# Attention weights turned on VectorE in squares of 32 and exchanged through DRAM, in place of TensorE transposes

## The chip, the cores and the metric

The kernel runs on one core of one Trainium2 chip, as one program. The metric is the device time of one execution in microseconds (us); the median of three executions is given.

## What is computed

The reference has two layers over a tensor x of 8 x 256 x 256 (batch, sequence, width). Layer 0 is a mixture of experts inside another one (two expert networks, A and B). Layer 1 is attention followed by a third expert network (D). The change lies in the attention alone:

```python
xn = layernorm(x, g_in)
q = (xn @ Wq).reshape(b, n, H, DH).transpose(0, 2, 1, 3) * scale      # 16 heads of 64
kv = xn @ Wkv                                                        # one key and value head for all
k = concatenate([nk, k], axis=1); v = concatenate([nv, v], axis=1)   # one null key in front
sim = einsum('bhid,bjd->bhij', q, k) + bias                          # bias: one 256 x 256 table per head
sim = where(causal_mask, neg, sim); sim = where(mask_p, sim, neg)
attn = softmax(sim, axis=-1)
out = einsum('bhij,bjd->bhid', attn, v)
return layernorm(out.reshape(b, n, INNER) @ Wo, g_out)
```

## The kernel before

Every instruction of every engine is written out by hand; engines meet through semaphores. The attention runs over 8 batches (b) and, in each, over 8 pairs of heads (j); p = 8b + j counts the 64 pairs. One pass of the inner loop is called a slot here: each engine has a fixed program for slot p, in `pe_batch`, `act_batch`, `dve_batch` and `pool_batch` (TensorE, ScalarE, VectorE, GpSimd).

A pair has two heads (o = 0, 1) and two blocks of 128 queries (i). Because of the causal mask the first block needs 129 keys (the null key and 128) and the second 257; a score row of both has 386 columns. The steps of a pair are these:

- `pe_queries` makes the queries of the pair (2 matmuls of 256 columns into psY), `act_queries` copies them to `c_qr`.
- `pe_scores` makes the scores (4 matmuls into psH), `dve_scores` adds the bias and mask tile `c_bm` (made by GpSimd in `pool_bm`) and takes the minimum of each row, for one head at a time (two custom instructions and two reads of the accumulator). The same kind of pass is done for the other head.
- `act_exp` makes the exponentials `c_p` and their sums. `dve_sums` takes reciprocals of the 4 sums per partition.
- The weighted sum over keys needs the weights with keys on partitions. `pe_turn` transposes three 128 x 128 pieces for each head on TensorE (psHT), `act_pT` and `dve_pT` copy them out, one head each, to `c_pT`.
- `dve_over` spreads the reciprocals over 64 columns for each head (`c_over`), and two more transposes in `pe_queries` turn them. They ride in the upper half of psY and of `c_qr`.
- `pe_sum` multiplies the values `c_v` with `c_pT` (4 matmuls into psL), `dve_o` multiplies by the turned reciprocals, and `pe_out` multiplies with `Wo` into psM (2 matmuls that add up over the pairs of a batch).

In slot p TensorE does sum(p-1), scores(p+1), turn(p), queries(p+2) with the turned reciprocals of p, out(p-1). Besides these, each slot of a batch has work of its own: row statistics and normalization of the next batch (slots 2 and 3), its keys and values (slots 5, 6), the output rows of the batch before, and the routing of network D (from batch 2 on). SP (SyncE) issues the loads; at the start of the attention it queues all weights of D and the zeroing of D's rows in DRAM.

## Time and profile before

| | us |
|---|---|
| median of 3 executions | 797.87 |
| lowest, highest | 794.5, 798.69 |
| span of the profiled execution, first to last instruction | 793.7 |
| attention, first slot to the last weighted sum (344.51 to 655.21) | 310.7 |

The time of the profiled execution itself is not listed apart from the three; its span lies 0.8 us under the fastest of them and 4.2 us under the median. In the rows below, "busy" is the time in which an engine had an instruction in its pipeline. Instructions of one engine overlap a little, so what one costs is read from the start of one to the start of the next.

### The profile page before, as it was taken

To read this page: it belongs to the slowest core of one execution; us is meant where nothing else is said; L and a number is where in the kernel's file an instruction comes from. 1 tells how busy PE (TensorE), PEld (TensorE's weight loads), DVE (VectorE), ACT (ScalarE), POOL (GpSimd) and SP (SyncE) were. 2 spreads that over 40 slices of the span, in tenths; PEclk is the share of its full clock that TensorE was granted. 3 is DMA by queue.
4 is the path that set the end of the run, shared out by engine and by line. 5 is a ranking of instruction groups with operands and counts; after the bars stand their busy time and mean duration, and the time that the engine had idled before them with its cause. 6 is when DMAs were issued, how large, how long until landed. Compare 5 with 4: busy or idle time off the path is not lost. (4 is left out here: it accounts for less than half of the span.)

```text
span 793.7 us, 16690 instructions
## 1 busy us (share of the span) xinstructions
PE 748.7 (94%) x4993; PEld 595.9 (75%) x4994; DVE 453.7 (57%) x1647; ACT 381.9 (48%) x1094; POOL 422.4 (53%) x506
## 2 busy tenths in 40 slices
PE   8889999769999999989999999999999988899998
PEld 4479966549999999867777777777777754699965
DVE  0824475672232323356666787778878787256557
ACT  3556612242222222166666565656666651777611
POOL 1077327525554852274656668686868356056640
PEclk9999999759999999999999999999999999999999
DMA  9636635429897773395000000000000001356547
GB/s 323 279 108 191 137 118 160 126 81 342 309 329 273 223 231 121 107 401 174 28 1 28 2 28 29 28 29 28 29 1 29 1 29 63 102 160 177 153 149 236
DMA packets 57022, 106.36 MB, mean 134 GB/s; under 512 B 8816, under 2 KB 42864, under 8 KB 55792
## 3 DMA queue, kind: packets, MB, share of 16 engines
q1 hardware_dynamic: 40368, 55.96, 20.9%
q0 software_dynamic: 10944, 30.03, 12.5%
q10 hardware_dynamic: 5632, 19.41, 7.2%
q8 instruction: 39, 0.64, 0.3%
q14 instruction: 39, 0.32, 0.1%
HBM read 78.31 MB, written 27.07 MB: 133 GB/s over the span
## 5 line engine op out<-in xcount | busy, mean ns | idle before, releaser
L2135 POOL TENSOR_TENSOR work<-work,region_ac 128x386 f32<-128x386 f32 x128 | 120.3, 945 | 67.2 <-DVE work L1797 32.7
L1683 ACT ACTIVATE work<-work 128x129 f32<-128x129 f32 (+1 forms) x256 | 114.0, 449 | 5.8 <-DVE work L1797 5.8
L1797 DVE CUSTOM_DVE_ANT_0 work<-psH,work 128x129 f32<-128x129 f32 (+1 forms) x256 | 78.8, 345 | 2.6 <-PE psH L1482 2.6
L1690 ACT COPY work<-psHT 128x384 f32<-128x384 f32 x64 | 30.6, 479 | 86.4 <-PE psHT L1492 86.4
L1355 POOL DMA_INDIRECT d_pairs<-work,home x47 | 46.1, 981 | 42.8 <-DVE home_f L1107 27.4
L1463 PE MATMUL psY<-work,region_ac 128*128 128x256 f32 x256 | 66.9, 384 | 0.5 <-ACT work L1677 0.5
L1516 PE MATMUL psM<-region_ac,work 128*128 128x256 f32 x256 | 66.0, 380 | 0.0
L1025 ACT ACTIVATE work<-work 128x512 f32<-128x512 f32 x39 | 24.6, 630 | 86.0 <-DVE work L1044 86.0
L1344 POOL DMA_INDIRECT b_pairs<-work,home x39 | 38.0, 975 | 49.8 <-DVE work L1051 46.8
L1336 POOL DMA_INDIRECT work<-in_x,inv x39 | 37.0, 949 | 47.0 <-DVE inv L1264 35.5
L848 PE MATMUL psH<-work,region_bd 128*128 128x128 f32 x472 | 59.2, 280 | 2.0 <-ACT region_bd L747 1.1
L1482 PE MATMUL psH<-region_bd,work 64*128 64x129 f32 (+1 forms) x512 | 59.4, 350 | 1.4 <-DVE work L1797 1.4
L848 PEld LDWEIGHTS psH<-work,region_bd 128*128 128x128 f32 x472 | 56.5, 196 | 2.8 <-ACT work L956 1.4
L1492 PEld LDWEIGHTS psHT<-ident,work 128*128 128x128 f32 x384 | 40.8, 141 | 21.2 <-issue 20.3
L1492 PE MATMUL psHT<-ident,work 128*128 128x128 f32 x384 | 56.1, 282 | 0.0
L1505 PE MATMUL psL<-work 128*64 128x256 f32 (+1 forms) x512 | 55.7, 339 | 0.1
L1336 POOL DMA_INDIRECT work<-y_scratch,inv x39 | 37.6, 965 | 32.2 <-DVE inv L1264 20.7
L1505 PEld LDWEIGHTS psL<-work 128*64 128x64 f32 x512 | 31.2, 136 | 30.3 <-issue 21.1
L1677 ACT ACTIVATE work<-psY 128x512 f32<-128x512 f32 (+1 forms) x66 | 38.5, 583 | 29.9 <-PE psY L1468 24.4
L1823 DVE TENSOR_TENSOR work<-psL,work 128x256 f32<-128x256 f32 x64 | 26.9, 421 | 44.6 <-PE psL L1505 44.3
L1417 POOL DMA_INDIRECT work<-a_slots,slot_u x32 | 31.1, 973 | 33.4 <-DMA a_slots<-work 23.9
L1683 ACT ACTIVATION_READ_ACCUMULATOR work<-work 128x1 f32 x256 | 48.7, 190 | 0.0
(368 smaller groups left out, 1694.6 us busy)
## 6 DMA issues: line engine op xcount, KB each, us to landing
region_bd<-in_b_w ACTq DMA_DIRECT2D x37, 512.0 KB, 5.4
work<-d_rows SPq DMA_DIRECT2D x47, 132.0 KB, 2.2
a_slots<-work SPq DMA_DIRECT2D x19, 256.0 KB, 2.9
region_bd<-in_b_w SPq DMA_DIRECT2D x1, 4096.0 KB, 15.3
work<-b_pairs SPq DMA_DIRECT2D x16, 256.0 KB, 3.1
region_bd<-in_d_w SPq DMA_DIRECT2D x1, 4096.0 KB, 13.2
work<-d_pairs SPq DMA_DIRECT2D x16, 256.0 KB, 4.3
d_rows<-region_bd SPq DMA_DIRECT2D x1, 2112.0 KB, 28.5
```

What stands on the lines that cost most here:

```text
L848: last = pe.matmul(pair_h[p % DEEP][:, t % PAIR, j, :], f.w_in(j, k, t), xT[:, p % DEEP, t % PAIR, k, :], start=(k == 0), stop=(k == KD - 1))
L1336: pool.indirect_dma_start(out=slot_rows(f, t), out_offset=None, in_=st.src, in_offset=bass.IndirectOffsetOnAxis(ap=inv[:, t:t + 1], axis=0 ...
L1355: pool.indirect_dma_start(out=st.pair_dram, out_offset=bass.IndirectOffsetOnAxis(ap=home[:, t:t + 1], axis=0), in_=d_ys[:, t % ROWS, :], i ...
L1463: last = pe.matmul(psY[:, 0:SEQ], c_wq[:, c, j * P:(j + 1) * P], c_xnT[:, odd, c, :], start=(c == 0), stop=(c == KD - 1))
L1482: last = pe.matmul(psH[:, o, a:z], c_qr[half, j % 2, i * P:(i + 1) * P], c_kT[half, 0:z - a], start=True, stop=True)
L1492: last = pe.transpose(psHT[:, o, n * P:(n + 1) * P], c_p[:, o, at:at + P], ident[:, :])
L1505: last = pe.matmul(psL[DH * o:DH * o + DH, queries], c_v[:, keys, :], c_pT[:, o, at], start=(n == 0), stop=(n == 1))
L1516: last = pe.matmul(psM[:, i * DIM:(i + 1) * DIM], c_oT[:, j % 2, i * P:(i + 1) * P], c_wo[:, j, :], start=(j == 0 and i == 0), stop=(j == ...
L1677: nc.scalar.mul(c_qr[:, j % 2, a:z], psY[:, a:z], -(float(DH) ** -0.5)).then_inc(C.qr_ready, 1)
L1683: nc.scalar.activation(c_p[:, o, a:z], c_sc[:, o, a:z], ACT.Exp, scale=-1.0, bias=c_min[:, o, i:i + 1], accum_out=c_sum[:, j % 2, o, i:i + ...
L1797: last = nc.vector.tensor_tensor_reduce(c_sc[:, o, a:z], psH[:, o, a:z], c_bm[:, 2 * (j % 2) + o, a:z], 1.0, -LOWEST, ALU.add, ALU.min, c_ ...
L2135: pool.tensor_tensor(c_bm[:, 2 * (j % 2) + o, :], c_mp, c_bias[:, 2 * j + o, :], ALU.subtract).then_inc(C.bm_ready, 1)
```

## The change

The six transposes of the weights, the two of the reciprocals, their PSUM banks and the copies out of PSUM go away. VectorE now turns squares of 32 x 32 within each group of 32 partitions (`dve_blocks`, one instruction of 384 columns for each head; `dve_recs`, 256 columns of reciprocals). This gives turned squares that still lie in the wrong group of partitions. One DMA writes the whole pair (4 KB per partition, 512 KB) to DRAM, and another reads it back so that the squares land in the right group (`sp_store_blocks`, `sp_load_blocks`). The keys are held in another order for this (every fourth key together), so bias and mask arrive permuted. The weighted sum comes three slots later (LAG = 3), scores have two banks instead of one (psH and psHT in turn), the heads are taken in the order 1, 0, and D's weights are loaded differently: `d_w13` by SP, the others by ScalarE's queue in the first twelve slots, `d_b2` after the attention, since its room holds the buffers `c_x1` and `c_x2`. Rows of pairs (`c_gat`) are now loaded by ScalarE's queue too.

```diff
@@ pe_queries
-            if live(k, -2, 1 << 30):
-                wait(pe, C.rec_ready, k - 1)
-                for i in range(QT):
-                    last = pe.transpose(psY[:, SEQ + i * P:SEQ + (i + 1) * P], c_over[:, i, :, :].rearrange("p o n -> p (o n)"),
-                                        ident[:, :])
@@ pe_turn
-        def pe_turn(pe, p):
-
-            for o in range(2):
-                pe.wait_ge(C.p_ready, 4 * p + 2 * o + 2)
-                wait(pe, C.pT_ready[o], p)
-                for n, at in enumerate((1, KEYS0 + 1, KEYS0 + 1 + P)):
-                    last = pe.transpose(psHT[:, o, n * P:(n + 1) * P], c_p[:, o, at:at + P], ident[:, :])
-                last.then_inc(C.p_turned, 1)
@@ pe_sum
-            for s in C.pT_ready:
-                pe.wait_ge(s, p + 1)
+            wait_dma(pe, C.blocks_loaded, 0, p)
@@ pe_batch
-                before = not (first and j == 0)
-                if before:
-                    pe_sum(pe, p - 1, (j - 1) % NPAIR, b - (j == 0))
+                s = p - LAG
                 if not (last and j == NPAIR - 1):
                     pe_scores(pe, p + 1, (j + 1) % NPAIR, b + (j + 1) // NPAIR)
-                pe_turn(pe, p)
+                if s >= 0:
+                    pe_sum(pe, s, s % NPAIR, s // NPAIR)
...
-                if before:
-                    pe_out(pe, p - 1, (j - 1) % NPAIR, b - (j == 0))
+                if s >= 0:
+                    pe_out(pe, s, s % NPAIR, s // NPAIR)
@@ act
-        def act_pT(act, p):
-            act.wait_ge(C.p_turned, 2 * p + 1)
-            wait(act, C.pv_mm, p)
-            nc.scalar.copy(c_pT[:, 0, :], psHT[:, 0, 0:3 * P]).then_inc(C.pT_ready[0], 1)
@@ dve
         def dve_sums(dve, p, j):
             dve.wait_ge(C.p_ready, 4 * p + 4)
-            nc.vector.reciprocal(c_rec, c_sum[:, j % 2, :, :]).then_inc(C.rec_done, 1)
-
-        def dve_over(dve, p):
+            wait(dve, C.blocks_turned, 3 * p)
+            nc.vector.reciprocal(c_rec, c_sum[:, j % 2, :, :].rearrange("p o i -> p i o").unsqueeze(3).to_broadcast([P, QT, 2, 16])
+                                 ).then_inc(C.rec_done, 1)
+
+        def dve_recs(dve, p):
+
 
             dve.wait_ge(C.rec_done, p + 1)
...
+            nc.vector.transpose(out=c_x1[:, p % 2, :, 2 * (QT + 1):, :].rearrange("p b i q -> p i b q"),
+                                in_=c_rec.rearrange("p i o n -> p i (o n)").unsqueeze(2).to_broadcast([P, QT, 4, 32])
+                                ).then_inc(C.blocks_turned, 1)
+
+        def dve_blocks(dve, p, j, o):
+
+
+            n = ORDER.index(o)
+            dve.wait_ge(C.p_ready, 4 * p + 2 * n + 2)
+            if p >= 2 and n == 0:
+                wait_dma(dve, C.blocks_stored, 0, p - 2)
+            nc.vector.transpose(out=c_x1[:, p % 2, :, (QT + 1) * o:(QT + 1) * (o + 1), :].rearrange("p b i q -> p i b q"),
+                                in_=c_p[:, j % 2, o, 1:1 + BLOCK].rearrange("p (i b q) -> p i b q", b=4, q=32)).then_inc(C.blocks_turned, 1)
@@ sp
+        def sp_store_blocks(sp, p):
+
+
+            r = p % 4
+            sp.wait_ge(C.blocks_turned, 3 * p + 3)
+            if p >= 4:
+                wait_dma(sp, C.blocks_loaded, 0, p - 4)
+            sp.dma_start(blocks_dram[r].rearrange("a (k b) m -> (a k) (b m)", b=4), c_x1[:, p % 2, :, :, :].rearrange("p b n q -> p (b n q)")
+                         ).then_inc(C.blocks_stored.sems[p % 2], 16)
+
+        def sp_load_blocks(sp, p):
+
+
+            r = p % 4
+            wait_dma(sp, C.blocks_stored, 0, p)
+            wait(sp, C.o_ready, p - 1)
+            sp.dma_start(c_x2[:, p % 2, :, :, :].rearrange("p a n q -> p a (n q)"), blocks_dram[r].rearrange("a s m -> s a m")
+                         ).then_inc(C.blocks_loaded.sems[p % 2], 16)
...
+            sp_clear_rows(sp)
+            sp.dma_start(d_w13, io["d_w13"]).then_inc(D.weights_loaded, 16)
+            pairs = NPAIR * BATCH
+            for p in range(pairs):
+                sp_store_blocks(sp, p)
+                if p >= 1:
+                    sp_load_blocks(sp, p - 1)
+            sp_load_blocks(sp, pairs - 1)
```

How the instructions stand on VectorE in a slot of the middle (slot 2 of a batch), before. "ISA" is the score pass of `dve_scores` and its accumulator reads; the names in brackets are the semaphores waited for.

```order
L1823 TENSOR_TENSOR work<-psL,work 128x256 [waits c_wo_mm,c_qr_ready,c_pv_mm]
L1803 RECIPROCAL work<-work 128x4 [waits c_p_ready,c_bm_ready,c_s_mm]
L1797 ISA work<-psH,work 128x129
L1797 ISA work 128x1
L1797 ISA work<-psH,work 128x257
L1797 ISA work 128x1
L1809 COPY region_bd<-work 128x256 [waits c_qr_mm,c_rec_done]
L1815 COPY work<-psHT 128x384 [waits c_p_turned,c_pv_mm,b_combined,c_out_step]
L1797 ISA work<-psH,work 128x129
L1797 ISA work 128x1
L1797 ISA work<-psH,work 128x257
L1797 ISA work 128x1
```

And the same place of the changed kernel, from the start of the slot to its second score pass.

```order
L1835 STREAM_TRANSPOSE region_bd<-work 128x3x4x32 [waits tokens_stored0,c_p_ready]
L1810 ISA work<-psHT,work 128x129 [waits c_p_ready,c_bm_ready,c_s_mm]
L1810 ISA work 128x1
L1810 ISA work<-psHT,work 128x257
L1810 ISA work 128x1
L1835 STREAM_TRANSPOSE region_bd<-work 128x3x4x32 [waits c_p_ready]
L1817 RECIPROCAL work<-work 128x64 [waits c_blocks_turned,c_p_ready]
L1824 STREAM_TRANSPOSE region_bd<-work 128x2x4x32 [waits c_rec_done]
L1844 TENSOR_TENSOR work<-psL,region_bd 128x256 [waits c_wo_mm,tokens_stored3,c_pv_mm]
```

The multiplication by the reciprocals (L1823, now L1844) moved from the start of the slot to behind the turning; the reciprocal has 64 columns instead of 4.

TensorE in one slot before, from the weighted sum to the output.

```order
L1505 MATMUL psL<-work 64x256 [waits c_o_ready,c_pT_odd,c_pT_even]
L1505 MATMUL psL<-work 64x256
L1505 MATMUL psL<-work 64x128 x2
L1482 MATMUL psH<-region_bd,work 128x129 [waits c_score_ready,c_kT_ready,c_qr_ready]
L1482 MATMUL psH<-region_bd,work 128x129
L1482 MATMUL psH<-region_bd,work 128x257 x2
L1492 MATMUL psHT<-ident,work 128x128 [waits c_pT_even,c_p_ready]
L1492 MATMUL psHT<-ident,work 128x128 x2
L1492 MATMUL psHT<-ident,work 128x128 [waits c_pT_odd,c_p_ready]
L1492 MATMUL psHT<-ident,work 128x128 x2
```

TensorE in one slot of the changed kernel, from the scores to the output, which is the last thing of the slot.

```order
L1487 MATMUL psHT<-region_bd,work 128x129 [waits c_score_ready,c_qr_ready]
L1487 MATMUL psHT<-region_bd,work 128x129
L1487 MATMUL psHT<-region_bd,work 128x257 x2
L1500 MATMUL psL<-region_bd,work 64x256 [waits c_o_ready,tokens_stored3]
L1500 MATMUL psL<-region_bd,work 64x256
L1500 MATMUL psL<-region_bd,work 64x128 x2
L1473 MATMUL psY<-work,region_ac 128x256 [waits c_qr_ready]
L1473 MATMUL psY<-work,region_ac 128x256
L1511 MATMUL psM<-region_ac,work 128x256 [waits c_o_ready]
L1511 MATMUL psM<-region_ac,work 128x256
```

The scores now stand ahead of the weighted sum, and right behind the output of the slot before, which waits for VectorE's `dve_o` (c_o_ready).

## Rows read from the trace of the kernel before

**Rows 1.** The page: span, and busy time of each engine.

```profile
span 793.7 us, 16690 instructions
PE 748.7 (94%) x4993; PEld 595.9 (75%) x4994; DVE 453.7 (57%) x1647; ACT 381.9 (48%) x1094; POOL 422.4 (53%) x506
```

**Rows 2.** Windows of batches 0, 2, 4, 7: length; busy PE, PEld, DVE, ACT, POOL; clock; DMA.

```profile
344.51:382.46 37.95, 37.71 (x270) 27.15 (x272) 23.13 (x103) 25.29 (x90) 23.94 (x31) 1.00 0.63 232
...
420.13:459.13 39.00, 39.00 (x286) 29.20 (x288) 28.67 (x129) 24.27 (x85) 24.31 (x33) 1.00 0.05 15
...
498.65:538.18 39.53, 39.36 (x289) 29.34 (x291) 31.76 (x137) 24.43 (x85) 28.50 (x37) 1.00 0.09 28
...
617.22:655.21 37.99, 35.36 (x263) 25.77 (x264) 28.92 (x129) 21.61 (x74) 18.72 (x22) 1.00 0.05 16
```

**Rows 3.** Timeline of TensorE through one slot: start, length, instructions merged.

```profile
452.57 0.44 PE L1468 MATMUL psY<-ident,region_bd 128*128 128x128 f32 x2
452.84 1.03 PE L1516 MATMUL psM<-region_ac,work 128*128 128x256 f32 x4
453.80 0.87 PE L1505 MATMUL psL<-work 128*64 128x256 f32 x8
454.60 0.93 PE L1482 MATMUL psH<-region_bd,work 64*128 64x129 f32 x8
455.46 0.88 PE L1492 MATMUL psHT<-ident,work 128*128 128x128 f32 x6
456.17 1.03 PE L1463 MATMUL psY<-work,region_ac 128*128 128x256 f32 x4
```

**Rows 4.** Timeline of VectorE in one slot (the reads of accumulators left out).

```profile
451.00 0.18 DVE L1803 RECIPROCAL work<-work 128x4 f32<-128x4 f32 x1 [0.43 <-PE psH L1482]
451.09 0.26 DVE L1797 CUSTOM_DVE_ANT_0 work<-psH,work 128x129 f32<-128x129 f32 x1
...
451.62 0.42 DVE L1776 COPY region_bd<-psX 128x256 f32<-128x256 f32 x1
...
451.96 0.55 DVE L1809 COPY region_bd<-work 128x256 f32<-128x256 f32 x1
...
452.43 0.55 DVE L1815 COPY work<-psHT 128x384 f32<-128x384 f32 x1
...
452.90 0.28 DVE L1797 CUSTOM_DVE_ANT_0 work<-psH,work 128x129 f32<-128x129 f32 x1
```

**Rows 5.** Groups of VectorE by form, whole span and attention: busy, mean ns.

```profile
L1803 DVE RECIPROCAL work<-work 128x4 f32<-128x4 f32 x64 | 11.3, 176 | 21.4 <-PE psH L1482 19.7 <-ACT work L1683 1.5
...
L1998 DVE RECIPROCAL home_f<-home_f 128x16 f32<-128x16 f32 x1 | 0.3, 253 | 0.0
...
L1809 DVE COPY region_bd<-work 128x256 f32<-128x256 f32 x64 | 29.2, 457 | 0.0
```

**Rows 6.** Timeline of VectorE in slot 3 of batch 4.

```profile
515.23 0.17 DVE L1842 TENSOR_SCALAR out_rstd<-out_mv 128x2 f32<-128x2 f32 x1
...
517.23 1.68 DVE L1938 TENSOR_TENSOR prev<-prev,oh 128x16 f16<-128x16 f16 x2
518.83 0.41 DVE L1823 TENSOR_TENSOR work<-psL,work 128x256 f32<-128x256 f32 x1
```

**Rows 7.** DMA from 353 to 363 us; then two transfers from 383 on; a first issue.

```profile
DMA packets 1603, 3.55 MB, mean 355 GB/s; under 512 B 336, under 2 KB 1318, under 8 KB 1474
...
work<-b_pairs SPq DMA_DIRECT2D x2, 256.0 KB, 4.0
...
333.55 1.64 SPq L2278 DMA_DIRECT2D work<-b_pairs  x2
```

**Rows 8.** End of the attention on VectorE; exponentials of ScalarE, from the page.

```profile
650.40 0.42 DVE L1797 CUSTOM_DVE_ANT_0 work<-psH,work 128x257 f32<-128x257 f32 x1
...
655.21 0.42 DVE L1823 TENSOR_TENSOR work<-psL,work 128x256 f32<-128x256 f32 x1 [0.91 <-PE psL L1505]
...
L1683 ACT ACTIVATE work<-work 128x129 f32<-128x129 f32 (+1 forms) x256 | 114.0, 449 | 5.8 <-DVE work L1797 5.8
```

More of the change, by code:

```diff
@@ L28 @@
 KEYS0, KEYS1 = 1 + P, 1 + SEQ
+BLOCK = QT * P + P
+PIECE = (2 * BLOCK + SEQ) // 4
+ORDER = (1, 0)
+LAG = 3
 KEYS = KEYS0 + KEYS1
@@ L1443, in build @@
         first_pair = Use(tokens_stored, 1)
+        C.blocks_stored = Use(RingOf((tokens_stored, 0, 2)), NPAIR * BATCH)
+        C.blocks_loaded = Use(RingOf((tokens_stored, 2, 4)), NPAIR * BATCH)
+        tokens_stored.count = C.blocks_stored.after + C.blocks_loaded.after
         def pe_null(pe):
@@ L1501, in pe_sum @@
             wait(pe, C.o_ready, p)
-            for n, keys, queries in ((0, 0, slice(0, SEQ)), (1, 1, slice(P, SEQ))):
-                at = slice(n * SEQ, n * SEQ + queries.stop - queries.start)
+            weights = c_x2[:, p % 2, :, 0:2 * (QT + 1), :].rearrange("p a (o i) q -> p o i a q", o=2)
+            for n, queries, blocks in ((0, slice(0, SEQ), slice(0, QT)), (1, slice(P, SEQ), slice(QT, QT + 1))):
                 for o in range(2):
-                    last = pe.matmul(psL[DH * o:DH * o + DH, queries], c_v[:, keys, :], c_pT[:, o, at],
-                                     start=(n == 0), stop=(n == 1))
+                    last = pe.matmul(psL[DH * o:DH * o + DH, queries].rearrange("p (i a q) -> p i a q", a=4, q=32),
+                                     c_v[:, b % 2, n, :], weights[:, o, blocks, :, :], start=(n == 0), stop=(n == 1))
             last.then_inc(C.pv_mm, 1)
@@ L1632, in pe_batch @@
                 over = (j + 2) // NPAIR
-                pe_queries(pe, p + 2, (j + 2) % NPAIR, (odd + over) % 2, None if last and over else b + over)
-                if before:
-                    pe_out(pe, p - 1, (j - 1) % NPAIR, b - (j == 0))
+                if not (last and over):
+                    pe_queries(pe, p + 2, (j + 2) % NPAIR, (odd + over) % 2, b + over)
+                if s >= 0:
+                    pe_out(pe, s, s % NPAIR, s // NPAIR)
         def batches(eng, batch):
@@ L1692, in act_zT, with act_load_pairs @@
+        def act_load_pairs(act, b):
+            wait(act, B.combined, 2 * b)
+            for i in range(QT):
+                act.dma_start(c_gat[:, i, :, :], pair_rows(B, 2 * b + i)).then_inc(C.pairs_loaded, 16)
         def act_zT(act, b):
@@ L2036, in dve_batch @@
                 p = 8 * b + j
+                s = p - LAG
                 more = not (last and j == NPAIR - 1)
-                if not (first and j == 0):
-                    dve_o(dve, p - 1, j + 1)
+                dve_blocks(dve, p, j, ORDER[0])
                 dve_dispatch_start(dve, b, j, last)
@@ L2098, in dve_attention @@
             dve_scores_wait(dve, 0)
-            for o in range(2):
+            for o in ORDER:
                 dve_scores(dve, 0, 0, o)
             batches(dve, dve_batch)
-            dve_o(dve, NPAIR * BATCH - 1, NPAIR - 1)
+            for j in range(NPAIR - LAG, NPAIR):
+                dve_o(dve, NPAIR * (BATCH - 1) + j, j)
             dve_key(dve, BATCH - 2, psX)
@@ L2170, in pool_z @@
         def pool_z(pool, b):
+            if b == 0:
+                pool.wait_ge(D.zeroed, 16)
             if b >= 2:
@@ L2205, in pool_batch @@
                 over = (j + 2) // NPAIR
-                for o in range(2):
-                    h = 2 * j + o
+                for n, o in enumerate(ORDER):
+                    h = 2 * j + n
                     if h <= 2 * QT and not last:
                         pool_pairs_wait(pool, b + 1, h)
-                    if j == 4 and o == 0:
+                    if j == 4 and n == 0:
                         pool.wait_ge(C.xn_ready, 2 * b + 2)
-                    if j == 6 and o == 1 and not first:
+                    if j == 6 and n == 1 and not first:
                         pool.wait_ge(C.z_step, 2 * b)
@@ L2256, in pool_attention @@
             for p in range(2):
-                for o in range(2):
+                for o in ORDER:
                     pool_bm(pool, 0, p, p, o)
```

214 lines of the change are left out of this document (111 added, 103 removed).

## The prediction

> **What bounds the kernel now.** I read the page first: the span is 793.7 us and TensorE is busy for 94% of it, VectorE for 57% [rows 1]. That is an average over three networks and the attention, so I cut the attention into its batches. The eight windows from 344.51 to 655.21 add up to 310.7 us. In each but the last TensorE is busy for the whole window to within 0.3 us, at a granted clock of 1.00, while VectorE is busy for 23 to 32 us of 38 to 39.5 and ScalarE for about 24 [rows 2]. So TensorE is the bound of the attention, and VectorE has room: little from batch 3 on (31.8 of 39.5), more before. The timeline says what TensorE's time goes to. From start to start, a slot takes 0.27 us for the turned reciprocals, 0.96 for the output, 0.80 for the weighted sum, 0.86 for the scores, 0.71 for the six transposes and about 0.97 for the queries (by the output, which has the same shape) [rows 3]: 4.57 us, or 36.6 in a batch. The other 3 us of a full batch are rows, keys and values, and routing.
>
> **What the change takes from TensorE.** The eight transposes: 0.71 + 0.27 = 0.98 us in each slot. The rest is 3.59 us, with the extra work 28.7 + 3 = 31.7 in a full batch, against 39.5. If TensorE stayed the bound, this would be worth 0.98 x 64 = 63 us. The question is what comes next.
>
> **What it does to VectorE.** Durations are from start to start. A score pass of one head (129 and 257 columns with their accumulator reads) is 451.09 to 451.62 = 0.53. A pass over 256 columns that moves one column per step is 451.62 to 451.96 = 0.34, one over 384 columns 452.43 to 452.90 = 0.47, and the reciprocal of 4 columns 0.09 [rows 4]. Slot before: two score passes 1.06, dve_o 0.34, reciprocal 0.09, copy of the turned weights 0.47, spreading copy 0.38 (mean 0.457 busy, of which some 0.08 overlaps the next [rows 5]). Sum 2.34, or 18.7 in a batch.
>
> No 32 x 32 turn is in the trace. Its nearest rows are the copies with the same number of columns: 0.47 and 0.34 [rows 4]. As a lower bound I take half of that (two columns per step), as an upper bound twice. I take the copies' price, since a turn reads and writes every column once. The reciprocal of 64 columns is not there either, but two sizes are: 4 columns take 176 ns and 16 take 253 [rows 5], that is 6.4 ns for each further column, six times a copy's. 48 more columns give 253 + 308 = 560 ns. The turn of the reciprocals waits for its result, so I count 0.60 up to its start. The bounds are 0.25 (no growth beyond 16) and 0.75.
>
> The Trainium skill has a reason for this slope: "VectorE: DVE Perf Modes", in its walkthrough of the 8-slice pipeline, says that the reciprocal is an iterative division with a repeat count of 8, at 0.96 GHz. By this rule a column costs 8.3 ns, 64 of them 0.69 us with the base of the row, and my sum would rise by 0.13 x 64 = 8 us; the rows say 6.4 ns.
>
> Slot after: two turns 0.94, two score passes 1.06, reciprocal 0.60, its turn 0.34, dve_o 0.34 = 3.3 us, that is 26.3 in a batch against 18.7. In batch 4 all other work of VectorE is 31.76 - 18.7 = 13.1 us [rows 2]; it stays. 26.3 + 13.1 = 39.4 us: VectorE alone now needs as long as the batch takes today.
>
> **The loop of a slot.** By the order of instructions, scores(p+2) on TensorE stand behind out(p-3), which waits for dve_o(p-3). dve_o stands on VectorE behind score pass, turn, reciprocal and turn of the same slot, and the next slot's first score pass waits for scores(p+2). Once round: score pass 0.53, turn 0.47, reciprocal 0.60, turn 0.34, dve_o 0.42, wake 0.1, output 0.96, scores 0.93 to their end [rows 3, 4], wake 0.05: 4.4 us. No slot can be shorter than this, though TensorE has work for 3.6 only. Before, TensorE ran transposes between the two, and there was no such idle time.
>
> **Batches after.** Eight slots at 4.4 are 35.3 us. A slot has room for 1.1 us of other work on VectorE (4.4 - 3.3); what exceeds this is added. Slot 3 has by far the most. Its normalization part alone runs from 515.23 to 518.83 = 3.6 us, of which 0.8 waits for GpSimd and 1.7 is one addition of 2 x 16 columns that takes that long beside GpSimd's work [rows 6]. With the output rows (now here too, 0.7, and statistics 0.7) it has 4.8 us, 3.7 too much. Slots 2, 4, 5, 6 exceed by about 0.3 each. A full batch is 35.3 + 3.7 + 1.2 = 40.2 against 39.5. The early batches have fewer extras (VectorE is busy for 23.1 and 28.7 us in batches 0 and 2): 36.4, 37.5, 38.8 against 37.95, 37.67 (the gap between the windows of 0 and 2), 39.00 [rows 2]. In the last batch the last score pass ends after three slots of 4.4, then 5.1, 4.6, 6.8 (slot 5 has two rounds of routing) and 4.3, that is 34.0; before, it ended at 650.8, which is 33.6 [rows 8]. Together: -1.6 - 0.2 - 0.2 + 4 x 0.7 + 0.4 = **+1.2 us**. The 63 us of TensorE are thus eaten by the loop and by VectorE.
>
> **The exchange.** 0.52 MB in two transfers landed 4.0 us after issue, and the DMA engines move 355 GB/s when they have a queue [rows 7], 1.5 us for 0.52 MB. A slot moves 1.05 MB, 3 us of 4.4, so bandwidth is enough. The load of p is issued after dve_o(p-2), and the sum of p comes two slots later less 2.4 us: 2 x 4.4 - 2.4 = 6.4 us. I take 4.0 + 1.5 (the store queued just ahead) = 5.5; it is hidden with 0.9 to spare. The cover is thin: above 6.4 every slot grows by half the excess.
>
> "DMA: Bandwidth & Descriptors" of the Trainium skill gives 2.0 us plus bytes over 436 GB/s for a transfer (its anatomy of one DMA, for the software path), so 3.2 us for 0.52 MB. By it the drain below would be 1.6 us shorter; the row says 4.0.
>
> **The two ends.** At the end nothing hides the exchange. Before, the last dve_o starts 4.4 us after the last score pass [rows 8]. After it: exponentials 1.2 (two of 0.449, accumulator reads and wake [rows 8]), turn, reciprocal, turn 1.4, store 3.7 to 4.0, load 4.0, weighted sum 0.87 = 11.4. That is **+7**. At the start, store 0 queues on SP behind pair rows, zeroing and d_w13: 0.5 + 2.2 + 4.2 MB from 333.55 on, plus three pieces of ScalarE's queue, 7.7 MB at 355 GB/s = 22 us [rows 7], to 355.3; store 0 lands at about 357.5. VectorE wants its buffer in slot 2, at 344.5 + 2 x 4.4 = 353.5. That is **+4**. The late load of d_b2 (2 MB, 6 us) runs beside the routing of D and costs nothing; without that cover it would be 6. ScalarE loses a copy and half of another and stays far from the bound.
>
> **Sum.** +1.2 + 7 + 4 = +12.2 us, made against the span of 793.7: 805.9. The median is 4.2 above this span: 810.
>
> **Rivals.**
> - *VectorE lighter than I count* (other side): the reciprocal costs 0.25 instead of 0.60, or the turns run at half the price, or the addition in slot 3 is no longer held by GpSimd. The reciprocal alone shortens loop and load by 0.35 x 64 = 22 us: 788. It decides from 0.2 us per slot on (12.2 / 64). For it: only two points fix the slope. Against: both agree with one line through a base of 0.15. Chance 0.19.
> - *Little change*: half of this, or drain and head hidden; 794 to 802. Chance 0.12.
> - *The forecast*: VectorE and the loop bound, own range 802 to 820. Chance 0.46.
> - *The exchange is late*: the round takes 8 us instead of 5.5, because writing and reading share 16 engines. Then a slot is (8 + 2.4) / 2 = 5.2, and seven slots of eight grow, some partly: 0.6 x 56 = +34, 844. For it: 5.5 is pieced together from transfers that had no other beside them. Against: bandwidth. Chance 0.12.
> - *Turns at twice the price*: +0.81 in the slot's loop and +1.28 in VectorE's load, +52 to +80 us, 862 to 890. Nothing in the trace excludes it. Chance 0.08.
> - *TensorE's clock falls to 1.2 GHz* now that it waits in each slot: it was 1.00 with 93% busy in the last batch [rows 2], lower shares there are none in the attention. Each slot would lose about 1.5 us. Chance 0.03.
>
> **Range and chances.** 0.5%, 4 us, is what a measurement of this kernel can tell from no change. Faster 0.19, within 0.12, slower 0.69. The range reaches from the first rival's 788 to 832, up to a mildly late exchange; it leaves out about 0.09 below and 0.13 above.
>
> **What would show it.** In the profile after: TensorE busy for 75 to 85% of the attention windows, VectorE for over 90%; the reciprocal at 0.56 us and the turns at 0.55 and 0.42 busy; TensorE's idle time before the output put down to dve_o, VectorE's before the first score pass to the scores; full batches of about 40 us; a gap of some 8 us between the last turn and the last sum. The forecast is wrong if full batches take under 38 us (VectorE's sum is off) or over 42 with waits on the DMA (the exchange is late).

## The result, and the profile after

| | before | after |
|---|---|---|
| median of 4 runs, us | 798.28 (794.5 to 798.94) | 823.66 (821.22 to 824.86) |
| span of the profiled execution | 793.7 | 822.8 |
| first score pass to last `dve_o` | 312.1 | 341.8 |

The ratio after / before is 1.0347, 95% interval 1.0296 to 1.0398. The change makes the kernel 25 us slower; forecast were 12. The spans of the two profiled executions differ by 29.1 us: before, the span of the profiled one lies near the fastest of the four times (794.5), after, the profiled one is the slowest (824.86). Here and below the ratios leave out executions more than 1.5% above the fastest of their kernel, and the one profiled of e10_clean was such a one (869.7 us, the other four 855.1 to 861.0). The third line is a stretch that this section and the experiments come back to: it starts with the first score pass (343.16 before, 341.48 after) and ends with the start of the last `dve_o` (655.21 in [rows 8], 683.23 after). It grew by 29.7 us, so the whole loss lies in the attention. The windows of [rows 2] start at 344.5 in both kernels, 1.7 us later from the first score pass in after than before; their sum grew by 28.0.

The page of after, its span, the busy times of the engines and the granted clock of TensorE in 40 slices:

```profile
span 822.8 us, 15606 instructions
PE 720.3 (88%) x4481; PEld 549.6 (67%) x4482; DVE 509.4 (62%) x1711; ACT 347.3 (42%) x1028; POOL 424.2 (52%) x506
PEclk9999999679999999969999999999998998999999
```

TensorE is busy for 28 us less than in [rows 1] and the span still grew. The windows of the batches in after, cut as in [rows 2] (batches 0, 3, 5, 6 and 7; columns as there):

```profile
344.50:383.91 39.41, 29.64 (x160) 19.20 (x160) 27.80 (x105) 18.75 (x74) 21.20 (x28) 0.78 0.88 309
...
465.47:507.41 41.94, 35.64 (x225) 23.16 (x223) 38.21 (x145) 20.13 (x77) 28.66 (x37) 0.96 0.69 227
...
550.32:592.30 41.98, 34.06 (x225) 22.40 (x223) 38.26 (x146) 20.13 (x77) 28.67 (x37) 1.00 0.70 227
592.30:637.10 44.80, 37.03 (x227) 23.99 (x225) 38.43 (x145) 20.12 (x77) 27.56 (x35) 0.92 0.62 201
637.10:683.23 46.13, 35.93 (x230) 22.59 (x226) 35.87 (x138) 16.96 (x64) 21.59 (x25) 0.96 0.69 228
```

In a full batch (3 to 6) TensorE is busy for 34 to 37 us (81 to 85%), VectorE for 38.2 to 38.4 (86 to 91%). Three things are to be seen. Full batches take 41.9 to 44.8 us, not the forecast 40.2. They have the same work (38.2 to 38.4 on VectorE) and yet differ by 3 us, and the longest has the lowest clock. And even the undisturbed ones, 3 and 5, are 1.8 too long.

**The loop of a slot.** TensorE from one output to the next (slots 0 and 1 of batch 3):

```profile
468.04 1.13 PE L1511 MATMUL psM<-region_ac,work 128*128 128x256 f32 x4 [0.88 <-DVE work L1844]
469.11 0.93 PE L1487 MATMUL psH<-region_bd,work 64*128 64x129 f32 x8
469.96 0.87 PE L1500 MATMUL psL<-region_bd,work 128*64 128x256 f32 x8
...
470.86 1.11 PE L1473 MATMUL psY<-work,region_ac 128*128 128x256 f32 x4
472.49 0.48 PE L1511 MATMUL psM<-region_ac,work 128*128 128x256 f32 x1 [0.53 <-DVE work L1844]
```

VectorE beside it, from the score pass to `dve_o` (L1844):

```profile
470.08 0.29 DVE L1810 CUSTOM_DVE_ANT_0 work<-psH,work 128x129 f32<-128x129 f32 x1 [0.65 <-PE psH L1487]
...
470.64 0.57 DVE L1835 STREAM_TRANSPOSE region_bd<-work 128x384 f32<-128x384 f32 x1
471.14 0.51 DVE L1817 RECIPROCAL work<-work 128x64 f32<-128x64 f32 x1
471.69 0.45 DVE L1824 STREAM_TRANSPOSE region_bd<-work 128x256 f32<-128x256 f32 x1
472.05 0.39 DVE L1844 TENSOR_TENSOR work<-psL,region_bd 128x256 f32<-128x256 f32 x1
472.36 0.28 DVE L1810 CUSTOM_DVE_ANT_0 work<-psH,work 128x129 f32<-128x129 f32 x1
```

The output starts at 468.04 and at 472.49: 4.45 us, and both engines wait in it, TensorE for `dve_o`, VectorE for the scores. The forecast said 4.4. From start to start a turn takes 0.50 (forecast 0.47), the reciprocal 0.55 (0.60), its turn 0.36 (0.34). The estimate from the Trainium skill's repeat count of 8 for the reciprocal (VectorE: DVE Perf Modes, the walkthrough of the 8-slice pipeline) is 0.69 us; the row has 0.51, so the slope read from two sizes of the trace was the better guide.

**Slots with other work.** The keys and values of the next batch on TensorE (L1528, L1532) in slot 5 of batch 3, up to the output behind them, and VectorE's score pass that waits for it:

```profile
493.05 1.13 PE L1528 MATMUL psX<-work,region_ac 128*128 128x256 f32 x4
494.01 1.05 PE L1532 MATMUL psX<-region_ac,work 128*128 128x128 f32 x8
494.90 1.03 PE L1473 MATMUL psY<-work,region_ac 128*128 128x256 f32 x4
495.77 1.03 PE L1511 MATMUL psM<-region_ac,work 128*128 128x256 f32 x4
```

```profile
497.70 0.29 DVE L1810 CUSTOM_DVE_ANT_0 work<-psHT,work 128x129 f32<-128x129 f32 x1 [0.62 <-PE psHT L1487]
```

Keys and values take 493.05 to 494.90 = 1.85 us. With TensorE's 3.6 that slot is about 5.4 us long on TensorE alone, and VectorE waits. The forecast had spread this work over the batch.

**Clock.** TensorE in slots 3 to 5 of batch 4:

```profile
530.12 0.63 PE L1522 MATMUL psX<-ident,work 128*128 128x128 f32 x4 [2.65 <-DVE region_bd L1890]
530.59 1.61 PE L1473 MATMUL psY<-work,region_ac 128*128 128x256 f32 x4
532.30 2.08 PE L1511 MATMUL psM<-region_ac,work 128*128 128x256 f32 x4
534.31 0.93 PE L1487 MATMUL psH<-region_bd,work 64*128 64x129 f32 x8
```

After a wait of 2.65 us the same output that takes 1.03 to 1.13 elsewhere takes 2.08: TensorE's lower level, 1.2 GHz. The window of that batch has a granted clock of 0.96. In the attention before, the clock was 1.00 in all eight windows (four of them are in [rows 2]). The lowest one after is 0.78, in batch 0, where TensorE stands still during VectorE's wait for the block buffer (below); what it costs there is counted with the head of the attention.

**The two ends.** VectorE waits in slot 2 of the first batch for the block buffer, and the last batch ends so (second half of the last score pass, last turn, store, the last sums and the last `dve_o`):

```profile
356.12 0.58 DVE L1835 STREAM_TRANSPOSE region_bd<-work 128x384 f32<-128x384 f32 x1 [6.80 <-DMA c_blocks<-region_bd]
```

```profile
670.79 0.42 DVE L1810 CUSTOM_DVE_ANT_0 work<-psHT,work 128x257 f32<-128x257 f32 x1
...
673.32 0.45 DVE L1824 STREAM_TRANSPOSE region_bd<-work 128x256 f32<-128x256 f32 x1
673.79 0.32 SPq L2317 DMA_DIRECT2D c_blocks<-region_bd  x1
...
676.55 0.87 PE L1500 MATMUL psL<-region_bd,work 128*64 128x256 f32 x8 [0.71 <-DMA region_bd<-c_blocks]
...
682.31 0.87 PE L1500 MATMUL psL<-region_bd,work 128*64 128x256 f32 x8 [0.48 <-DMA region_bd<-c_blocks]
683.23 0.42 DVE L1844 TENSOR_TENSOR work<-psL,region_bd 128x256 f32<-128x256 f32 x1 [2.59 <-PE psL L1500]
```

From the end of the last score pass (671.21) to the start of the last `dve_o` it is 12.0 us; before it was 4.4 [rows 8], so the drain grew by 7.6. Store and load of the last pair take 673.79 to 682.31 = 8.5.

### The profile page after: what moved, and what is told of

Its sections match the earlier page's. It is cut to its first block and busy times, and to the rows that moved or that the text cites. A ratio compares the mean times of both kernels' runs of the same rounds, so it can differ in the third digit from the quotient of the medians.

```text
span 822.8 us, 15606 instructions
## 1 busy us (share of the span) xinstructions
PE 720.3 (88%) x4481; PEld 549.6 (67%) x4482; DVE 509.4 (62%) x1711; ACT 347.3 (42%) x1028; POOL 424.2 (52%) x506
## 5 line engine op out<-in xcount | busy, mean ns | idle before, releaser
L1511 PE MATMUL psM<-region_ac,work 128*128 128x256 f32 x256 | 75.1, 418 | 39.0 <-DVE work L1844 32.5
L1511 PEld LDWEIGHTS psM<-region_ac,work 128*128 128x128 f32 x256 | 46.4, 198 | 64.7 <-DVE work L1844 59.9
L1835 DVE STREAM_TRANSPOSE region_bd<-work 128x384 f32<-128x384 f32 x128 | 73.1, 571 | 7.4 <-DMA c_blocks<-region_bd 6.8
L856 PE MATMUL psH<-work,region_bd 128*128 128x128 f32 x472 | 59.4, 280 | 2.2 <-ACT region_bd L755 1.3
L1500 PE MATMUL psL<-region_bd,work 128*64 128x256 f32 (+1 forms) x512 | 58.0, 349 | 1.8 <-DMA region_bd<-c_blocks 1.8
L1500 PEld LDWEIGHTS psL<-region_bd,work 128*64 128x64 f32 x512 | 32.0, 140 | 34.8 <-issue 21.3
L1344 POOL DMA_INDIRECT work<-y_scratch,inv x39 | 37.6, 965 | 32.5 <-DVE inv L1272 21.0
L1473 PEld LDWEIGHTS psY<-work,region_ac 128*128 128x128 f32 x256 | 45.7, 199 | 11.0 <-issue 6.3
L1810 DVE CUSTOM_DVE_ANT_0 work<-psHT,work 128x129 f32<-128x129 f32 (+1 forms) x128 | 40.0, 348 | 16.2 <-PE psHT L1487 16.2
L1810 DVE CUSTOM_DVE_ANT_0 work<-psH,work 128x129 f32<-128x129 f32 (+1 forms) x128 | 39.8, 347 | 15.6 <-PE psH L1487 15.6
L2223 POOL DMA_INDIRECT d_rows<-region_bd x32 | 32.3, 1011 | 19.7 <-DVE region_bd L1955 13.5
L909 PE MATMUL psH<-work,region_bd 128*128 128x128 f32 x320 | 40.5, 282 | 0.0
```

Of the source, the lines that this page charges most:

```text
L856: last = pe.matmul(pair_h[p % DEEP][:, t % PAIR, j, :], f.w_in(j, k, t), xT[:, p % DEEP, t % PAIR, k, :], start=(k == 0), stop=(k == KD - 1))
L909: last = pe.matmul(ffn_h[u % RING][:, j * P:(j + 1) * P], f.w_in(j, k, u % RING), b_xT[:, u % 2, k, :], start=(k == 0), stop=(k == KD - 1))
L1344: pool.indirect_dma_start(out=slot_rows(f, t), out_offset=None, in_=st.src, in_offset=bass.IndirectOffsetOnAxis(ap=inv[:, t:t + 1], axis=0 ...
L1473: last = pe.matmul(psY[:, 0:SEQ], c_wq[:, c, j * P:(j + 1) * P], c_xnT[:, odd, c, :], start=(c == 0), stop=(c == KD - 1))
L1500: last = pe.matmul(psL[DH * o:DH * o + DH, queries].rearrange("p (i a q) -> p i a q", a=4, q=32), c_v[:, b % 2, n, :], weights[:, o, block ...
L1511: last = pe.matmul(psM[:, i * DIM:(i + 1) * DIM], c_oT[:, j % 2, i * P:(i + 1) * P], c_wo[:, j, :], start=(j == 0 and i == 0), stop=(j == ...
```

## Experiments

The executions for the experiments ran on other chips, on which the kernel before takes 839 to 845 us; so each kernel is given by its ratio to the kernel before on its own chip. The interval of a ratio is some +-0.5%, 4 us. The second column is finer: the stretch from the first score pass to the last `dve_o` in one profiled execution, which is 341.75 in the changed kernel on the first chip and 341.84 on another.

| kernel | ratio (95%) | stretch, us |
|---|---|---|
| before | 1 | 312.1 |
| changed kernel | 1.035 (1.030 to 1.040) | 341.8 |
| e8_after, the same again | 1.039 (1.033 to 1.044) | 341.8 |
| e1_narrow | 1.021 (1.017 to 1.026) | 327.1 |
| e2_defer | 1.029 (1.024 to 1.034) | 329.2 |
| e3_keep | 1.040 (1.035 to 1.045) | 342.5 |
| e4_head | 1.033 (1.027 to 1.039) | 337.8 |
| e5_end | 1.034 (1.029 to 1.038) | 337.8 |
| e6_fill | 1.039 (1.034 to 1.043) | 339.6 |
| e7_three | 1.017 (1.012 to 1.023) | 323.8 |
| e9_best | 1.000 (0.996 to 1.004) | 313.3 |
| e10_clean | 1.020 (1.015 to 1.026) | 333.9 |
| e11_spread | 0.996 (0.993 to 1.000) | 307.7 |
| e12_nofill | 0.997 (0.994 to 1.001) | 307.1 |

Two theories were to be told apart. One: a slot is set by the loop from `dve_o` over out and scores back to VectorE. Its rival: VectorE's own load sets it. Beside them stood two suspected costs, head and clock.

**e8_after.**

> The changed kernel once more, unedited, on the chip of the others, so that they can be held against it directly. Ratio to before 1.03 to 1.04, from first score pass to last dve_o 342 us; batches 3 and 5 at 41.9, some others up to 3 us more.

Measured 1.039 and 341.8. Batches 3 and 6 took 41.9 here and batches 4 and 5 44.6 and 42.9; in the first execution 3 and 5 were the short ones and 4 and 6 took 42.9 and 44.7. So which batch is disturbed differs between executions, the sum hardly does.

**e1_narrow: reciprocal on 16 columns.** Shortened; the buffer `c_rec` shrinks with it.

```
-nc.vector.reciprocal(c_rec, c_sum[...]...to_broadcast([P, QT, 2, 16]))
+nc.vector.reciprocal(c_rec, c_sum[...]...to_broadcast([P, QT, 4, 2]))
-in_=c_rec.rearrange("p i o n -> p i (o n)").unsqueeze(2).to_broadcast([P, QT, 4, 32])
+in_=c_rec.rearrange("p i b o -> p (i b o)").unsqueeze(2).to_broadcast([P, QT * 4 * 2, 16])
```

> The reciprocal of the sums works on 16 columns instead of 64; the turn spreads them by reading each one 16 times. Nothing else changes. The reciprocal stands both in the loop of a slot and in VectorE's own load, so both theories (the loop sets a slot; VectorE's load sets it) expect the same: by the rows of before and after, 509 ns falls to about 253, 0.26 us per slot, 16 us in all, 807 us. If something else sets the slots by now (TensorE at a lower clock, the exchange), the time stays within 4 us of 824.

The reciprocal in the groups of e1_narrow:

```profile
L1817 DVE RECIPROCAL work<-work 128x16 f32<-128x16 f32 x64 | 13.5, 210 | 0.0
```

509 ns became 210, and every slot that was 4.45 became 4.15. The stretch is 14.7 us shorter and not 64 x 0.30 = 19. Most of the difference is one slot of batch 1 that took 7.7 us instead of 4.15: there TensorE waits 2.62 us for a load of blocks and then runs at its lower clock. Slots that TensorE sets (slot 5, 5.34) don't shrink either. That the total comes near the expected 16 is partly luck, since the reciprocal fell by more than expected (to 210 ns, not 253) and the late load took it back. Per column the reciprocal costs (509 - 210) / 48 = 6.2 ns, close to the 6.4 of the forecast.

**e2_defer: out behind the scores.** Shortened; the output that is left over is made behind the last batch.

```
 pe_scores(pe, p + 1, ...)
+if s >= 1: pe_out(pe, s - 1, ...)
 if s >= 0: pe_sum(pe, s, ...)
 ...
 pe_queries(pe, p + 2, ...)
-if s >= 0: pe_out(pe, s, ...)
```

> out(p-3) goes one slot later on TensorE, behind scores(p+2), so that the scores no longer wait for dve_o. VectorE's instructions and their order are the same. Loop theory: slots of 4.45 us fall to what VectorE needs, 3.4 to 3.7 us in a slot without other work; a batch falls to VectorE's busy time plus its waits for its own results, about 39 instead of 42, so 20 to 25 us less, 800 us. Load theory (VectorE is busy for 38.3 of 42 us in a full batch and can't go faster): at most 5 us less, 819 to 824.

The stretch fell by 12.6 us, between the two theories. The idle time that TensorE spends waiting for `dve_o` ahead of out fell from 32.5 us to 3.5, so the old loop is gone. But full batches fell by 1.4 only, to 40.5, and the light slots went from 4.45 to 4.32, not to 3.6. TensorE in e2_defer:

```profile
433.71 1.13 PE L1511 MATMUL psM<-region_ac,work 128*128 128x256 f32 x4
434.77 0.87 PE L1500 MATMUL psL<-region_bd,work 128*64 128x256 f32 x8
435.57 1.13 PE L1473 MATMUL psY<-work,region_ac 128*128 128x256 f32 x4
437.17 0.93 PE L1487 MATMUL psHT<-region_bd,work 64*128 64x129 f32 x8 [0.47 <-ACT work L1676]
```

Now queries, their scaling on ScalarE and the scores stand in a row with nothing between, and TensorE waits there. In the changed kernel the output stood in that gap. One wait was exchanged for another. What the full batches say is the second half: there the loop costs 1.4 of 42 us. Of the 40.5 that are left VectorE is busy for 37.9. The clock has a part in it too: in e2_defer it was 1.00 in all batches from 1 on, so some 4.4 of the 12.6 us are what the lower clock cost the changed kernel (e6_fill below), and the move itself is worth about 8.

**e5_end: the same, at the end of the slot.** In place of out(p-3) stands out(p-4), with no other move.

> out goes one slot later as in e2_defer, but stays at the end of the slot, between the queries and the scores that wait for them: in slot p TensorE does scores(p+1), sum(p-3), queries(p+2), out(p-4). If the slots of 4.32 us in e2_defer come from queries, ScalarE's scaling and scores in a row with nothing between, they fall to TensorE's 3.6 to 3.7 us; from the first score pass to the last dve_o the attention then takes about 321 us (342 in the changed kernel, 329 in e2_defer), 20 us less than the changed kernel on the same chip. The full batches stay at 40.5 us, since VectorE sets them. Rival: the 4.32 come from VectorE or GpSimd; then 329, as in e2_defer. The exchange has only 2 x 3.65 - 2.4 = 4.9 us in such slots; if it takes the 5.5 that I forecast, waits for DMA appear ahead of the weighted sums and slots stay near 4.

Light slots did fall to 3.58, so the reading of the 4.32 was right. The stretch did not follow: 337.8, not 321. Three things took it back. First VectorE now waits for the later out before the output rows (0.62 us per batch, the row at 509.36 below). Secondly, TensorE's waits gather into one, in slot 4, and the clock falls in nearly every batch (0.92 to 0.96 in the windows of batches 1 to 6). Thirdly, the exchange becomes late in the fast slots: TensorE's idle time ahead of the weighted sums put down to the DMA is 10.5 us (1.8 in the changed kernel). VectorE, then TensorE in batch 3, and the group of the sums:

```profile
509.36 0.76 DVE L1854 TENSOR_TENSOR acc<-psM,work 128x256 f32<-128x256 f32 x2 [0.62 <-PE psM L1511]
```

```profile
515.65 0.81 PE L1522 MATMUL psX<-ident,work 128*128 128x128 f32 x4 [4.67 <-DVE region_bd L1891]
516.25 1.91 PE L1473 MATMUL psY<-work,region_ac 128*128 128x256 f32 x4
517.96 1.73 PE L1511 MATMUL psM<-region_ac,work 128*128 128x256 f32 x4
```

```profile
L1500 PE MATMUL psL<-region_bd,work 128*64 128x256 f32 x256 | 43.2, 417 | 12.2 <-DMA region_bd<-c_blocks 10.5 <-DVE work L1845 1.6
```

**e4_head: d_w13 later.** In 16 pieces of 0.26 MB, one per slot from 8 to 23, in place of one load ahead of store 0.

> d_w13 (4.2 MB) is not issued by SP ahead of store 0, but in 16 pieces in slots 8 to 23. The queue ahead of store 0 is then 0.5 + 2.2 MB. VectorE's wait of 6.8 us for the block buffer in slot 2 should fall away: 6 to 7 us less, 817 us, and batch 0 about 33 us instead of 39.4. Rival: the wait only moves (the pieces delay exchanges of batches 1 and 2, or batch 1 was as late for another reason), and the time falls by less than 3 us.

The first eight slots, from the first score pass to that of slot 8, took 34.3 us instead of 39.1: 4.8 from the head. Batch 1 grew by 0.6, the stretch fell by 4.0. So the head cost 4.8 us (4 forecast), less than the 6.8 that the row shows: with the wait gone, the slot with the normalization took 7.95 us instead of 6.08.

**e3_keep and e6_fill: TensorE kept at work.** Both add transposes of a constant into a bank of scores that is free at the time; nothing reads them. e3_keep has six in each slot, ahead of out:

```
+pe.wait_ge(C.score_ready, 2 * p + 2)
+for _ in range(6):
+    pe.transpose(psS[j % 2][:, 0, 0:P], ident[:, :], ident[:, :])
 pe_out(pe, s, ...)
```

e6_fill has 14 in slot 3 ahead of out and 8 in slot 4 ahead of the rows, and none elsewhere.

> Six transposes of a constant in each slot (about 0.1 us each at full clock), ahead of out(p-3), where TensorE waits for dve_o, so that it is idle for less. If TensorE's lower clock costs what I read from the trace of after (batches 2, 4 and 6 longer by 0.6, 1 and 2.9 us than batch 3), the granted clock stays at 1.00 in the attention and the time falls by 4 to 6 us, 818 to 820. Rival: slots that fall behind are late for another reason (additions on VectorE that take long beside GpSimd's work), and the time stays within 2 us of 824 though the clock stays up. If the filling itself gets in the way, the time grows by up to 10.

> The changed kernel with 14 transposes of a constant in slot 3 ahead of out and 8 in slot 4 ahead of the rows, the two places where TensorE waits for longest for VectorE, and none elsewhere. If those waits are what lets TensorE's clock fall, full batches take 41.9 to 42.0 us each (batches 4 and 6 had 42.9 and 44.7), the granted clock is 1.00 in all windows but the first, and the time is 4 to 5 us under that of the changed kernel. Rival: the clock falls all the same (it follows something else, such as the share of a longer stretch), and batches of 43 to 45 remain.

e3_keep was a miss: the stretch stayed (342.5). The filling stood in the way of slot 5, which TensorE sets (5.34 became 6.00 in batches 1 and 2), and two batches were still at 0.96. e6_fill settles it for the full batches. Its windows of batches 3, 4, 5 and 6, from score pass to score pass:

```profile
495.02:536.97 41.95, 36.37 (x248) 24.82 (x246) 38.20 (x145) 20.13 (x77) 28.64 (x37) 1.00 0.69 227
536.97:578.94 41.97, 36.37 (x248) 24.82 (x246) 38.21 (x146) 20.11 (x77) 28.64 (x37) 1.00 0.69 227
578.94:620.90 41.96, 36.36 (x248) 24.80 (x246) 38.21 (x146) 20.13 (x77) 28.64 (x37) 1.00 0.68 225
620.90:662.86 41.96, 36.36 (x248) 24.81 (x246) 38.21 (x145) 20.11 (x77) 28.62 (x37) 1.00 0.66 215
```

All four are alike to 0.02 us, with a clock of 1.00. Against them the changed kernel lost 0.7, 1.0 and 2.7 us in batches 2, 4 and 6: 4.4 in all. This is the price of the clock, and it comes in single slots behind a wait, not in each slot. (Batch 3 had 0.96 in the changed kernel and lost nothing.) The gain didn't reach the ratio: batch 0 took 3 us more in e6_fill (41.8 to slot 8, against 38.8), in a longer wait for the first store (7.3 us against 6.5) and in slots that have the filling too; the stretch fell by 2.2.

**e10_clean: head and clock together.** The pieces of d_w13 go out every second slot from 24 to 54, later than in e4_head; the filling is that of e6_fill without the 14 of batch 0.

> The changed kernel with nothing but its two disturbances taken away: the head (d_w13 in late pieces) and the fall of the clock (the filling of e6_fill, from batch 1 on). If these are the two terms and they add up, batch 0 takes 34.3 us, full batches 41.95 each at a clock of 1.00, and from first score pass to last dve_o 341.8 - 4.7 - 4.3 = 333 us; what is left of the loss against the kernel before (9 us more in the attention's batches, 8 in the drain) is VectorE's load and the loop. Rival: one of the two only moves (batches 1 and 2 longer again, as in e4_head, where batch 1 took 0.6 more).

Measured: 34.8 for the first eight slots, four full batches of 41.94 to 41.98 at 1.00, the stretch 333.9 where 333 was expected. The two terms add up to within about 1 us: together they are 7.9 where head and clock by themselves were put at 4.8 + 4.4. What is left against the kernel before is 333.9 - 312.1 = 21.8 us.

**e7_three: e1_narrow, e4_head and e5_end in one.**

> e1_narrow, e4_head and e5_end together. If loop, VectorE's load and head add up as I take them: 0.3 us less per slot where VectorE sets it (full batches 40.5 - 2.4 = 38.1), light slots at TensorE's 3.6, head 4.8 less; from first score pass to last dve_o 342 - 20 - 10 - 5 = 307 us, 35 less than the changed kernel, and a ratio of 0.99 to the kernel before. Rival: at 3.6 us a slot the exchange becomes the bound (waits for DMA ahead of the sums) and half of it is lost: ratio 1.01.

The rival came out: 1.017 and a stretch of 323.8. Batch 1 took 41.4 us, with slots of 5.7 and 6.0 while the pieces of the weights were moving; TensorE waited 8.6 us for the DMA ahead of the sums; and the clock was below 1.00 in batches 0 to 6.

**e9_best: the same with its side effects removed.** In short form, against e7_three:

```
-D_W13 pieces in slots 8 to 23            +every second slot from 24 to 54
+if s >= 1 and j == 3: pe_out(pe, s - 1, ...)      # behind the scores
 if s >= 0: pe_sum(pe, s, ...)
+if j == 4 and not last: 28 (batches 0, 1: 16) transposes of a constant
 ...
+if s >= 1 and j != 3: pe_out(pe, s - 1, ...)      # end of the slot
```

> All that the runs so far point to: reciprocal on 16 columns; out one slot later at the end of the slot, but in slot 3 behind the scores, so that the output rows don't wait for it (0.62 us in e5_end); 28 transposes of a constant (16 in batches 0 and 1) where TensorE waits 4.7 us in one piece in slot 4; d_w13 in pieces every second slot from 24 to 54, beside less traffic. Full batches: slots 4.4, 3.6, 3.6, 4.7, 8.05, 4.3, 5.34, 4.6, about 38.3 us, clock 1.00; batch 0 31.6, batches 1 and 2 about 36. First score pass to last dve_o about 305 us, 37 less than in the changed kernel, ratio to the kernel before 0.995. If the exchange (waits for DMA of 8.6 us in e7_three) is a bound of its own and not due to the weights' pieces, batches 1 and 2 stay at 40: 313 us, ratio 1.005.

Ratio 1.000 and a stretch of 313.3: as long as before. Batches 4 and 6 took 38.0 and 37.6 where 38.3 was expected. The rival's 313 us came out, but not as it had said: batches 1 and 2 took 37.9 and 36.9, not 40. The miss of 8 us is the exchange: TensorE's waits for it lie in the batches that came out too long, 3.1 us in batch 0, 3.4 in batch 1, 4.3 in batch 5. One load of blocks beside a piece of d_w13 is late by 3 us; the group says how much in all:

```profile
594.63 1.03 PE L1500 MATMUL psL<-region_bd,work 128*64 128x256 f32 x8 [3.02 <-DMA region_bd<-c_blocks]
...
L1500 PE MATMUL psL<-region_bd,work 128*64 128x256 f32 x256 | 42.7, 413 | 18.1 <-DMA region_bd<-c_blocks 17.3 <-DVE work L1853 0.4
```

**e11_spread and e12_nofill: the weights only where slots are long.** In short form, against e9_best; e12_nofill leaves out the filling as well.

```
-if 24 <= p < 56 and p % 2 == 0:          # SP, d_w13
+if p in [8b + 3, 8b + 4 for b in 1..7] + [45, 53]:
-if p < 8 ... elif p < 12                 # ScalarE's queue, d_w2 and small ones
+if p in [8b + 3, 8b + 5 for b in 1..6]:
```

> e9_best with the pieces of the weights (d_w13 on SP, d_w2 and the small ones on ScalarE) issued only in slots 3 and 4 (d_w13; two in slot 5) and 3 and 5 (ScalarE), the slots that VectorE or the keys and values make long. In e9_best TensorE waits 17.3 us for the DMA ahead of the weighted sums, 3.0 of it once behind a piece of d_w13. If the pieces cause this, the waits fall to under 6 us, batches 3 to 6 to 37.9 each and batch 0 and 1 by 2 us or so: from first score pass to last dve_o 305 us, 8 less than e9_best, ratio to the kernel before 0.99. If the exchange is too slow for slots of 3.6 us by itself, the waits stay above 12 us and the ratio at 1.00.

> e11_spread without the 28 (16) transposes of a constant in slot 4. By e5_end and e7_three TensorE's granted clock then falls after its wait of 4 to 5 us in slot 4, to 0.92 to 0.96 of a batch, and a batch grows by 1 to 2.5 us: 8 to 12 us longer than e11_spread from first score pass to last dve_o. Rival: the long waits cost nothing by themselves, since VectorE sets those slots: within 2 us of e11_spread.

e11_spread: waits for the DMA 11.8 us instead of 17.3, stretch 307.7, ratio 0.996. Both explanations hold in part: the pieces cost 5.5 us of waits, and the rest stays, so at 3.6 us a slot the exchange is late by itself now and then (a sum more than three slots behind was not tried). e12_nofill was a miss: the rival's number came out, but not its reason. The clock fell again (0.96 and 0.88 in batches 4 and 6, which took 40.1 and 42.8 us), but the filling costs about as much as it saves where the clock would have held, batch 2 among them (37.6 with it, 36.2 without), and the stretch is 307.1. So this filling is worth nothing in this version.

e11_spread and e12_nofill have the shortest stretch of all, 4 to 5 us under the kernel before, but their intervals reach 1.000 and 1.001. No version was found that is certain to beat the kernel before.

## Why the prediction was right and wrong

The direction held, and so did the mechanism: TensorE is relieved, then VectorE and the loop set the slots. The size, +12, was less than half of the measured +25. The step that failed is the sum of the batches, +1.2. By its own steps:

- **TensorE frees 0.98 us per slot and stops being the bound.** Right. Busy 36 us of 42, and it waits for VectorE.
- **The loop of a slot is 4.4 us.** Right in size (4.45), and e2_defer shows that it is out that closes it. But it decides only light slots. In full batches it is worth 1.4 us; in the other 40.5 VectorE is busy for 37.9.
- **Prices of turns and reciprocal.** Right within 0.05 us each; e1_narrow confirms the slope per column. The rivals *turns at twice the price* and *VectorE lighter* fell by this. One reading was of a mixed mean: the spreading copy of [rows 5] has a mean of 457 ns but a median of 292 (last section). For the sum over a batch the mean is the right one.
- **Batches +1.2.** This is the step that failed. Undisturbed they are 11.2 us longer than before (28.0 between the sums of the windows, less 4.8 head, 7.6 drain and 4.4 clock). Each of the four full batches is 1.7 us above its forecast of 40.2, batches 1 and 2 are 1.9 and 1.5 above theirs. The term "slots 2, 4, 5, 6 exceed by about 0.3 each" was made from averages. Measured excesses over 4.45 for a full batch are 0.60 in slot 2, 3.88 in slot 3, 0.11, 0.78 and 0.67 in slots 4 to 6, and 0.29 behind slot 7: 6.3 us, where the forecast had 4.9. Of it, slot 5 is TensorE's: 1.85 us of keys and values can't hide in a slot whose idle time is 0.85. In slots 2 and 6 small VectorE operations stand beside GpSimd's additions and take long: the cast of slot 2 0.70 us, and in slot 6 an operation of 32 columns (L1905) 0.81, where the same line takes 0.23 in slot 4. That these make the rest is read from the rows; no run took them out. The 3.7 for slot 3 came close (3.88 measured), though its sum is off: 3.6 + 0.7 + 0.7 is 5.0 and not 4.8, which would have given 3.9.
- **Early batches 37.5 and 38.8.** 39.4 and, undisturbed, 40.3 (e6_fill): the same two causes, as slot 5 is 5.34 and slot 3 is 7.3 to 7.5 from batch 1 on.
- **Head +4, drain +7.** 4.8 and 7.6. Right.
- **The exchange is hidden.** Right for this kernel: 1.8 us of waits ahead of the sums, and 0.9 to spare was the right warning. With slots of 3.6 us (e5_end, e7_three, e9_best) it comes out, 9 to 17 us of waits.
- **TensorE's clock, chance 0.03, "each slot would lose about 1.5 us".** Too small a chance, and too coarse a picture. The argument was that TensorE would wait a little in each slot; it also waits 1.1 to 2.7 us at a time in slots 3 and 4, for VectorE's 3.9 us of extra work there, and single slots behind that ran at 1.2 GHz. In batch 3 the slow slot lay under VectorE's work and cost nothing (41.94 at 0.96); in batches 2, 4 and 6 it cost 4.4 us together.

Thus of the 15.8 us between the forecast and the measured windows, 10.0 are the batches, 4.4 the clock and 1.4 the two ends. With head and clock taken from e10_clean, which has them together (7.9), it is 11.3 for the batches, 3.9 for head and clock and 0.6 for the drain. Either way the batches are most of it.

The waits of [rows 6] also moved. The two additions of 16 columns (the forecast takes them for one) took 1.68 us together before and take 0.89 now; in their place the two row normalizations (L1781, 256 columns each) take 1.68, where they took 0.73. From the start of the first to the start of what follows the last it is 2.40 us instead of 2.25, and slot 3 came out at 8.33 where 8.1 was forecast.

## What to carry to other kernels

When a hand-ordered pipeline's bound moves to another engine, add up each slot by itself: the longest of the loop, each engine's own work *in that slot*, and its waits. Extra work that an average hides (1.85 us of keys and values, the normalization of slot 3) is paid for in the slot where it stands, with all that exceeds the idle time of that slot. Breaking a loop by moving one step opens the next one (queries, ScalarE, scores) and makes a hidden transfer visible, so such a move must be tried with its neighbours. And where an engine's idle time gathers in one place, look at the granted clock behind it.
